# Attention kernel on one core: the products with v of a group of four heads and half the queries issued in one unbroken run

## What is computed

```python
Qr, Kr = _rope(Qh, cos, sin), _rope(Kh, cos, sin)
scores = jnp.einsum('bhqd,bhkd->bhqk', Qr, Kr) * DH ** (-0.5)
scores = jnp.where(causal, jnp.finfo(scores.dtype).min, scores)
pattern = jax.nn.softmax(scores, axis=-1)
heads = jnp.einsum('bhqk,bhkd->bqhd', pattern, Vh).reshape(b, t, d)
return heads @ Wo.T
```

## Time and profile before

| | |
|---|---|
| runs, median of 3 | 1135.55 us (1133.46 to 1139.42) |
| profiled execution, span from the first to the last instruction | 1129.1 us (the page gives no time beside the span) |
| mean granted TensorE clock over the span | 0.931 |
| busy over the span: PE, DVE, ACT, POOL | 997.7, 796.5, 477.7, 399.6 us |
| attention of layer 0 | about 96 to 277 us |

### The profile page before, as it was taken

How to read it: one execution, slowest core, us unless ns; L and a number is a source line. 1 busy time by engine, 2 the same in 40 slices (tenths; PEclk the granted TensorE clock), 3 DMA queues, 4 the chain that set the end, 5 groups by cost and what they waited for, 6 DMA issues and landing times.

```text
span 1129.1 us, 17549 instructions
## 1 busy us (share of the span) xinstructions
PE 997.7 (88%) x5701; PEld 756.0 (67%) x5701; DVE 796.5 (71%) x1338; ACT 477.7 (42%) x981; POOL 399.6 (35%) x352
## 2 busy tenths in 40 slices
PE   4797999976777799989989998998999999899997
PEld 3684554533555677868777786776877778677775
DVE  4687665621578488678858958877885895887873
ACT  3322555553223345344434534535444453443542
POOL 2330001001045254444524525354452452535342
PEclk9895779776989899999999999999999999999999
DMA  5630111100030200200200200020020010001000
GB/s 218 213 97 1 49 41 31 31 1 21 11 102 19 71 24 10 66 24 10 65 24 0 50 26 23 10 65 24 10 65 24 1 51 25 24 10 46 15 1 37
DMA packets 19444, 46.17 MB, mean 41 GB/s; under 512 B 3032, under 2 KB 4704, under 8 KB 19104
## 3 DMA queue, kind: packets, MB, share of 16 engines
q1 hardware_dynamic: 19376, 45.43, 13.4%
HBM read 37.81 MB, written 7.61 MB: 40 GB/s over the span
## 4 chain that ended last, share of the span: by engine, by line
PE 40%; DVE 18%; issue 11%; DVEq 1%; DMA 1%; ACT 1%; POOL 0%; SPq 0%; ACTq 0%
PE bank L1535 11%; PE bank L1571 10%; PE bank L1662 7%; PE bank L1581 6%; PE bank L1557 4%; DVE d_pT_lo L1421 3%; DVE d_g_act L1260 2%; DVE d_neg_max L1308 2%; PE bank L1639 2%; DVE d_swap L1283 2%; DVE d_g_act L1256 2%; DVE d_swap L1281 1%; DVE d_rot L1281 1%; DVE d_rot L1283 1%; DMA d_vw_raw<-in_w_v 1%
## 5 line engine op out<-in xcount | busy, mean ns | idle before, releaser
L1471 POOL TENSOR_SCALAR d_probs<-d_probs,d_row_inv 128x1024 f32<-128x1024 f32 (+7 forms) x128 | 99.9, 782 | 230.2 <-DVE d_row_inv L1313 229.7
L1160 ACT ACTIVATE d_probs<-bank,d_neg_max 128x1024 f32<-128x1024 f32 (+7 forms) x128 | 95.3, 745 | 124.5 <-DVE d_neg_max L1308 122.1
L1421 DVE TENSOR_TENSOR d_pT_lo<-bank,d_pT_hi 128x512 fp32r<-128x512 f32 x192 | 99.0, 547 | 45.9 <-issue 28.2
L598 DVE TENSOR_REDUCE b_maxes<-bank 128x2 f32<-128x1024 f32 (+2 forms) x96 | 89.4, 956 | 35.1 <-PE bank L626 19.6
L1217 ACT CAST d_pT_hi<-bank 128x512 fp32r<-128x512 f32 x192 | 84.8, 482 | 64.9 <-PE bank L1639 64.7
L1535 PE MATMUL bank<-xT_hi,d_gu_hi 128*128 128x512 f32 x224 | 100.0, 447 | 11.7 <-DVE d_g_act L1256 5.7
L1639 PE MATMUL bank<-ident,d_probs 128*128 128x128 f32 x576 | 85.1, 279 | 21.5 <-DVE d_pT_lo L1421 18.9
L1308 DVE TENSOR_REDUCE d_neg_max<-bank 128x1 f32<-128x1024 f32 (+7 forms) x128 | 95.1, 748 | 11.2 <-PE bank L1584 10.9
L575 ACT ACTIVATE b_probsT<-bank 128x512 f32<-128x512 f32 x140 | 76.0, 593 | 45.8 <-PE bank L626 37.8
L1639 PEld LDWEIGHTS bank<-ident,d_probs 128*128 128x128 f32 x576 | 65.6, 142 | 42.4 <-DVE d_pT_lo L1421 28.2
L1535 PE MATMUL bank<-xT_hi,d_gu_lo 128*128 128x512 f32 x224 | 92.4, 413 | 0.0
(11 more groups left out here) (238 smaller groups left out, 2541.5 us busy)
## 6 DMA issues: line engine op xcount, KB each, us to landing
gu_raw<-in_gu SPq DMA_DIRECT2D x24, 256.0 KB, 2.7
d_cb<-comb_scratch SPq DMA_DIRECT2D x9, 512.0 KB
qk_raw<-in_w_qk SPq DMA_DIRECT2D x16, 256.0 KB, 5.8
d_ow_raw<-in_ow_b SPq DMA_DIRECT2D x8, 384.0 KB, 3.2
q_stack<-a_part_hi SPq DMA_DIRECT2D x4, 512.0 KB, 5.4
k_stack<-a_part_hi SPq DMA_DIRECT2D x4, 512.0 KB, 5.1
d_vw_raw<-in_w_v SPq DMA_DIRECT2D x8, 256.0 KB, 9.4
d_ow_raw<-in_ow_a SPq DMA_DIRECT2D x8, 256.0 KB, 9.4
```

Source lines behind the costliest of these rows:

```text
L598: nc.vector.tensor_reduce(maxes[:, p % 2, c, :, i], bank[:, first:first + 2, 0:w], AX_X, ALU.max, negate=True).then_inc(maxed, 1)
L1160: nc.scalar.activation(probs[s % NP_][:, 0:width(s)], score_bank(s, width(s)), ACT.Exp, bias=neg_max[:, h.col(s)], accum_out=row_sum[:, h. ...
L1421: nc.vector.tensor_tensor(pT_lo[c][:, j:j + blocks, col:col + P], bank[:, T_BANK + tu % 2, 0:blocks * P].rearrange("p (b q) -> p b q", b=b ...
L1471: nc.gpsimd.tensor_scalar(probs[s % NP_][:, 0:width(s)], probs[s % NP_][:, 0:width(s)], row_inv[:, h.col(s)], 1.0, ALU.mult, ALU.mult).the ...
```

## The change

Both values of MIX_STEP become zero, so all pieces of a group and half have one key, and TensorE issues them one after the other with no other step between. As mix_end holds MIX_STEP, the end of the pieces moves to an earlier key (by 0.09 for c = 0 and by 0.315 for c = 1), and with it all steps of the chain, on all four engines. The number of instructions, their operands and their waits stay as they are.

```diff
     MIX_AT = [1.5, 2.06]
-    MIX_STEP = [0.03, 0.045]
+    MIX_STEP = [0.0, 0.0]
 
     def mix_end(g, c):
         return 2 * g + MIX_AT[c] + (len(pv_pieces(c)) - 1) * MIX_STEP[c]
```

## The result

| | before | after |
|---|---|---|
| median of 4 runs | 1135.22 us (1133.46 to 1139.42) | 1151.34 us (1148.41 to 1155.68) |
| ratio after / before, 95% interval | | 1.0161 (1.0111 to 1.021) |
| span of the profiled execution | 1129.1 us | 1146.6 us |
| mean granted clock over it | 0.931 | 0.912 |

The change makes the kernel 1.6% slower. I had forecast 1140.6 us and a range up to 1146: the sign was right and the size a third of what came.

A forecast was written before the change was run, and what follows sets the result against it. TensorE was taken to set the pace at half clock and nearly so at full. Terms 1.2 + 0.3 + 1.8 + 1.0 + 0.7 = +5.0 us moved the span from 1129.1 to 1134.1, the median to 1140.6; range 1133 to 1146.

The forecast's parts named there:

- Round trips: On TensorE, 22 switches between score matmuls and products vanish, 0.22 us each: 4.8 us at full clock if nothing interferes.
- rival (c): Chance 0.07: TensorE bounds throughout, 5.8 us faster, 1129.7; needs waits before exp 4.4 and shift 5 under 1.4 us a group.
- Order: Waits from reordered steps, round trips included: 1.2 us first halves, 0.3 second halves, 0.7 group 3's tail.
- high and average are then behind us: Second half: these steps, formerly ahead of later exp steps, are already done, so the delay is mostly regained; loss 0.1 us a group.
- The clock: Attention groups: earlier falls of the clock cost 1.8 us, a late rise in one later group 1.0 us.
- its 4.3 us of first-half products run all at half: In one later group the clock rises too late: about 2 us more of half clock in dense work, costing 1.0 us.
- The other term of the clock: Behind the second half's products the clock falls 3.5 to 4 us earlier, costing 1.8 us over the groups.
- The base: Median taken as 1135.55 us, 6.4 above the profiled span, and moved by the same amount as the span.
- (a): Rival, chance 0.2: only the order costs, the clock's stretches stay the same relative to the work; 2.2 us slower, 1137.8.
- (d): Rival, chance 0.06: nothing is seen, VectorE and ScalarE make up for everything; 1135.5 us.
- (b): Rival, chance 0.17: second-half delays aren't regained and the clock rises late in three groups; 1145.1 us.

The follow-up runs named there:

- e3: Against the kernel before: both halves' products unbroken at the change's keys, the chain behind them kept at its old keys; 1134.78 us, ratio 1.0023.
- e1: Against the kernel before: only the first half's products unbroken, MIX_STEP = [0.0, 0.045]; 1147.1 us, ratio 1.0107.
- g1: Against the kernel before: all products unbroken as in the change, but the first half later, at 2g + 1.74; 1141.38 us, ratio 1.0076.
- g2: Against the kernel before: first half's products spread wider, second half unbroken with its early chain as in the change; 1133.88 us, ratio 1.0027.
- e2: Against the kernel before: only the second half's products unbroken, MIX_STEP = [0.03, 0.0]; 1141.53 us, ratio 1.0052.
- e7: Changed kernel plus four bf16 filler matmuls ahead of exp steps 5 to 8 of each second pair; 1156.46 us.
- f4: Changed kernel plus two fp32 filler products of v_all ahead of exp steps 5 to 8 of each second pair; 1158.6 us.
- f1: The kernel before, without edit, run again for a second trace of its clock; 1131.17 us.
- e5: The kernel before plus two bf16 filler matmuls ahead of each exp step; 1165.57 us.

## Why the prediction was wrong

**Round trips: the size is borne out.** 22 of them at 0.22 us were the first term; with the chain kept the kernel lies 4.0 us lower at equal clock, and the unbroken run of the second half took 5.73 us (139.81 to 145.54), forecast 5.6. They aren't isolated from the waits that changed with them. This is rival (c)'s gain, and it exists; the change throws it away in the place of its chain. The rule of the Trainium skill that a change of tiling mode drains the engine ("TensorEngine Tiling (Array Packing)", Tiling Modes) agrees with it.

**Order: the kind right, the size too small.** From the first product of group 0 to the first of its second half took 127.20 to 139.81, 12.61 us, against 168.41 to 180.10, 11.69, in the kernel before: +0.9 where I had +0.4. From there to group 1 it was 30.1 us against 29.2, +0.9 where I had +0.1 and 0.5 for the clock. Group 3's first half took 13.75 us and not 12.81: +0.9, forecast 0.7. The step that failed in c = 1 is "high and average are then behind us": the exp step behind the shift still waited 0.45 us as before, and the delay stayed. Over all runs the order costs 3.5 us; I had 2.2.

**The clock: the step that failed.** I had the group's start move past the moment at which the clock rises ("its 4.3 us of first-half products run all at half"), and it did, in group 1: rise at 173.83, 3.9 us after the first product. But I priced it as 2 us more of half clock, with the full clock holding from there to the end of the second half. It didn't hold: with the products over and sum waiting behind them, it fell again at 177.25 and stayed at half for 10.2 us, until 187.49. The time from the first product to the second half's went from 11.69 to 16.21 us, +4.5 instead of +1.4, and group 1 lasted 169.90 to 217.47, 47.6 us, instead of 40.95. Group 2, too, 46.84 instead of 40.22: the forecast had one such group, there are two, and the longer stretch at half behind the second half (20.5 us instead of 13.65) comes on top. Group by group the profile adds up: +1.8 + 6.6 + 6.6 + 0.9 = 15.9 of the 17.5 us. In all runs together it is (211.3 - 181.7) x 0.327 = 9.7 us by the clock and 3.5 by the order, 13.2. The split is an estimate: the line is one slope for half clock in dense work and in thin.

The other term of the clock, 1.8 us for a fall that comes 3.5 to 4 us sooner, failed too. In group 0 the clock fell at 156.77, 29.6 us after the group's first product as in the kernel before (198.01 after 168.41), although the last product ended 11.2 us ahead of the fall and not 7.8. That the products ended early didn't bring the fall forward there.

**The base.** I let the median stand 6.4 us above the span. What lies around the span is 1.8 us; the rest was that the profiled execution was one of the better runs.

**Rivals.** (a) fell, as the clock's stretches changed, and so did (d). (b), adding losses, named the rise late in three groups and was nearest with 1145.1, but had the same wrong price for it. (c) fell as a whole: the waits in front of exp 4.4 and shift 5 came to 1.6 us a group, over its point of 1.4.

**What is shown and what isn't.** Shown: unbroken products as such cost nothing (e3); the chain moved up behind the products costs 7.5 us in order and 28 us more at half clock (change against e3), and in group 0 of e1 and e3, one pair of traces, its place alone makes the difference between a clock that falls and one that stays up; closer halves or a spread first half take back most of the loss (g1, g2), and in groups 0 to 2 of g1 no stretch at half is left between the halves. Argued only: that a late rise does it. The rise came 3.9 us after the first product where the change lost the clock and 2.3 where it kept it, but e3 kept it at 3.1 and g1 at 3.7. Not shown is what in TensorE's work the clock follows. Most rises in the attention came with products running or just over, but not all: in e2 the clock rose at 184.53, 5.9 us after the last product and straight behind the 2.07 us of a spread step. Two kinds of filler didn't reliably hold it. "TensorE: Matmul & The Clock Gate" of the Trainium skill (Why this matters for your kernels) warns of long idle gaps between bursts; in this trace the clock stayed at half from 177.25 to 187.49 with TensorE busy 10.07 of 10.24 us, so that rule doesn't explain it.

## What to carry to other kernels

Before moving matmuls together, look where the granted clock rises and whether TensorE has work without waits behind the rise: a clock that comes up as the dense work ends can be lost again, and that cost more here (9.7 us, estimated) than the waits that I could count (3.5). Where a group of products is made unbroken, leave other work between it and the step that waits for its copy; here, at equal clock, the run alone gained 4 us and the moved chain lost 7.5. And a kernel at the edge of the clock has no single time: take many runs and set them against their mean clock before believing 1%.

## Hardware behaviour that I had not expected

- One unchanged kernel on one core ran from 1124.1 to 1156.1 us within 31 runs on one chip, with the mean granted clock between 0.938 and 0.898; 50 runs on three other chips stayed inside that range.
- TensorE stayed at half clock while busy 98% of 10.2 us (after, 177.25 to 187.49), 98% of 13.65 us in e7, 99% of 17.05 us in f4, and all of 10.24 us in f1.
- With the same rise at 130.32, the clock was lost 3.4 us later where TensorE was busy 2.71 of 3.42 us (e1) and stayed up where it was busy throughout (e3).
- Filler that took 31.7 us of TensorE in the trace cost 23 us at equal clock and left the mean clock where it was (e5: 0.917, the kernel before on the same chip 0.918).
